# Overlapping one sequence's chunk loop with the MLP of the one before and the in-projection of the next, and decays taken from running sums, in a Mamba-2 and mixture-of-experts layer

## Chip, cores and metric

One Trainium2 chip, one of its cores. The metric is the device time of one execution in microseconds; lower is better. All arrays are float32.

## What is computed

Input: 4 sequences of 512 tokens, 256 features each. Two residual blocks follow each other.

```python
# block 1, per sequence (Mamba-2 mixer, then an MLP with 704 hidden units)
x0 = layernorm(x);  h = rmsnorm(x0) * norm1_w
z, xBC, dt = split(h @ in_proj_w)               # 512, 768, 8 columns
dt  = softplus(dt + dt_bias)
xBC = silu(causal_conv(xBC, 4 taps) + conv_b)   # -> xs (8 heads x 64), B (128), C (128)
dA  = dt * -exp(A_log)
# chunks of 128 tokens:
L      = exp(segsum(dA))                        # 8 heads, 128 x 128, lower triangle
Y_diag = (C B^T * L) @ (xs * dt)
states = B^T @ (xs * dt * exp(A_last - A_cum))  # carried from chunk to chunk
Y_off  = (C @ state) * exp(A_cum)
y  = rmsnorm((Y_diag + Y_off + D * xs) * silu(z)) * mixer_norm_w
h1 = x0 + y @ out_proj_w
x  = x + h1 + (silu(h2 @ gate_w) * (h2 @ up_w)) @ down_w      # h2 = rmsnorm(h1) * norm2_w
# block 2: mixture of experts over all 2048 tokens, 8 experts, the best 2 for each token
x  = x + moe(layernorm(x))
```

## The kernel before

Five instruction streams (TensorE = PE, VectorE = DVE, ScalarE = ACT, GpSimd = POOL, SyncE = SP) are written by hand and meet in semaphores. Each engine works strictly in the order in which its stream is written. Tokens lie in tiles of 128 rows; a sequence has four of them, which are also its four chunks.

Block 1 runs in `body(b)`, once for each sequence, of which the two middle ones are a loop on each engine. Before the first body stands the in-projection of sequence 0 (`hT_`, `dt_`, `xbc_`, `z_`, `dec_` on PE). A body has two halves:

- The **chunk loop** over c = 0 to 3. PE: `seg_` (L434), `front` (transposes L358 and G = B C^T, L424), `off_` (L446, C times state), `back`'s eight products for the heads (L451), its state product (L459), `yT_` (transposes) and `out_` (L476). POOL's `masked_dA` (L1394) makes, for each chunk, a 128 x 1024 array, dA of each head masked by the triangle; `seg_` multiplies it by a triangle of ones, which gives the segment sums of all 8 heads in PSUM banks 4 and 5; ACT's `decay` (L787) takes the exponential into `em`; DVE's `front` (L1041, L1044) masks G and multiplies it in. DVE's `off` (L1050, L1052), `y_` (L1062), `state`, `h1_` (L1082, L1087, L1090) and POOL's `scaled_x` (L1399), `plus_x_D` (L1404), `gated` (L1410), `scale_y` finish the chunk.
- **In-projection of b + 1 and MLP of b.** `hT_`, `dt_` (L374), six `xbc_` (L391), `dec_` (L382), four `z_` (L402), then `h2T`, `mlp_up` (L543, L547, L552) and `mlp_down` (L566). Meanwhile ACT's `tap` and DVE's `conv_taps` (L1026, three instructions for each of 6 blocks) do the convolution, DVE's `dt_softplus` (L1006 to L1019) the softplus, DVE (L1255) the product of gate and up, and DVE's `add_mlp` the residual.

The routing of sequence b - 1 (`xn_`, logits, `route_pick`, `route_slots`, POOL's `scatter`) lies inside body b. The PSUM banks have several uses one after the other: banks 0 and 1 for instance hold z, dt, decays, states, y turned, the output product and the MLP. The experts' weights are loaded by SP: experts 0 and 1 right behind the other weights at the start, into a region of SBUF of their own; 2 to 5 as soon as the last sequence's chunk loop is over; 6 and 7 in block 2.

After block 1 come the last routing steps, the table of tiles, the first gather, and then 39 tiles of block 2 (L701 and L714 on PE, L1318 on DVE), in loops.

Of the kernel before, what the change touches and what calls it, by code (L numbers as in the profile page):

```python
# [7 lines left out]
P = 128  # L8
SEQS, SEQ = 4, 512
TOKENS = SEQS * SEQ  # L10
CH = SEQ // P
# [101 lines left out]
def build(nc, hidden, vecs, consts, empty, in_proj, out_proj, gate_w, up_w, down_w,  # L113
          router_w, w1, w2, w3, out):
    xn_rows = nc.dram_tensor("xn_rows", [TOKENS + P, D], F32).ap()
    lists = nc.dram_tensor("lists", [SLOT_TILES * P, 2], F32).ap()

    ctx = ExitStack()
    with ctx:
# [6 lines left out]
        at = [EARLY * EXPERT]  # L126
# [13 lines left out]

        win = cols(KD, PROJ)
# [3 lines left out]
        xc = cols(CB, SEQ)  # L145
        sz = cols(CH, INNER)
# [4 lines left out]
        bg = cols(2, 2 * P)  # L151
        gm = cols(2, P)
        mda = cols(2, HEADS * P)
        em = cols(2, HEADS * P)
# [17 lines left out]
        xnT = cols(KD, P)  # L172
        junk_h = cols(D)
        dec = cols(3, CH, HEADS)
        dtx, dta, dtu, dtd, dtr, dts, dts2, dtq, dtp, dtl, dtv, dA = (cols(CH, HEADS) for _ in range(12))
        st6 = cols(CH, 6)
        mv = cols(CH, 2)
        ve, rs, rr, t4a, t4b, cur_rs, ssy, ry, vy, ssh, rh, vh, ve2, rs2 = (cols(CH) for _ in range(14))
        cur_mv = cols(CH, 2)
        st6b = cols(CH, 6)  # L180
        mv2 = cols(CH, 2)
        late_end = at[0]
# [9 lines left out]
        ys = cols(D)  # L192
        at[0] = max(at[0], late_end)
# [25 lines left out]
        recg = cols(2 * P)  # L219
# [20 lines left out]


# [4 lines left out]
        cur_kept = sem("cur_kept")  # L246
# [1321 lines left out]
```

## Time and profile before

| | us |
|---|---|
| median of 3 runs | 812.43 |
| lowest, highest | 812.38, 813.51 |
| the profiled execution's own time | 808.96 |
| its span, first to last instruction | 807.1 |
| PE busy | 728.0 (90%) |
| DVE busy | 577.3 (72%) |
| POOL busy | 307.4 (38%) |
| ACT busy | 227.4 (28%) |

The profiled execution took 1.9 us more than its span, and 3.5 us less than the median. A view of the profile by stage gives busy time for each engine in a stretch; the chain of waits follows the last instruction back to what released it. A matmul of float32 shows as two records, a transpose as one. A record's duration holds its fill and drain, so that records overlap, and the distance between starts is the cost of one.

### The profile page before, as it was taken

To read this page: it belongs to the slowest core of one execution; us is meant where nothing else is said; L and a number is where in the kernel's file an instruction comes from. 1 tells how busy PE (TensorE), PEld (TensorE's weight loads), DVE (VectorE), ACT (ScalarE), POOL (GpSimd) and SP (SyncE) were. 2 spreads that over 40 slices of the span, in tenths; PEclk is the share of its full clock that TensorE was granted. 3 is DMA by queue.
4 is the path that set the end of the run, shared out by engine and by line. 5 is a ranking of instruction groups with operands and counts; after the bars stand their busy time and mean duration, and the time that the engine had idled before them with its cause. 6 is when DMAs were issued, how large, how long until landed. Compare 5 with 4: busy or idle time off the path is not lost.

```text
span 807.1 us, 10348 instructions
## 1 busy us (share of the span) xinstructions
PE 728.0 (90%) x2751; PEld 464.5 (58%) x2752; DVE 577.3 (72%) x1370; ACT 227.4 (28%) x482; POOL 307.4 (38%) x505
## 2 busy tenths in 40 slices
PE   5888999899998999979608999999999999999992
PEld 3466547664667547655504666666666666666661
DVE  4686827868477865853634888888888888888870
ACT  1654544544444534631102111111111111111110
POOL 1266203740456315532242333344433344333422
PEclk9999999999999999999758999999999999999997
DMA  9800001000010000038617211111211112111111
GB/s 324 293 2 1 1 0 53 2 0 0 2 52 0 0 0 27 26 120 274 181 31 276 47 32 26 27 26 29 35 28 26 26 26 32 32 26 26 26 15 19
DMA packets 30167, 43.74 MB, mean 54 GB/s; under 512 B 4099, under 2 KB 23875, under 8 KB 30128
## 3 DMA queue, kind: packets, MB, share of 16 engines
q1 hardware_dynamic: 21600, 33.15, 12.3%
q0 software_dynamic: 8544, 10.30, 8.0%
q8 instruction: 12, 0.20, 0.1%
q14 instruction: 11, 0.09, 0.0%
HBM read 33.84 MB, written 9.75 MB: 54 GB/s over the span
## 4 chain that ended last, share of the span: by engine, by line
PE 64%; DVE 11%; issue 9%; POOL 9%; DMA 3%; ACT 2%; DVEq 0%; POOLq 0%; ACTq 0%; SPq 0%
PE ps L701 28%; PE ps L714 14%; PE ps L391 5%; PE ps L402 3%; PE ps L547 3%; PE ps L358 3%; PE ps L552 3%; POOL lists L1426 2%; POOL big L1404 2%; DVE big L1318 2%; PE ps L476 1%; DVE big L1026 1%; PE ps L566 1%; PE ps L434 1%; PE ps L374 1%
## 5 line engine op out<-in xcount | busy, mean ns | idle before, releaser
L1318 DVE STREAM_TRANSPOSE big<-big 32x224 f32<-32x224 f32 x608 | 244.8, 403 | 9.1
L701 PE MATMUL ps<-big 128*128 x624 | 242.7, 542 | 1.1 <-ACT big L932 1.1
L701 PEld LDWEIGHTS ps<-big 128*128 128x128 f32 x624 | 119.0, 191 | 106.1 <-issue 104.1
L1361 POOL TENSOR_TENSOR big<-big 128x1 f32<-128x1 f32 x179 | 56.6, 316 | 280.3 <-DVE big L1326 159.5
L714 PE MATMUL ps<-big 128*128 x546 | 124.5, 380 | 2.1 <-DVE big L1338 1.3
L714 PEld LDWEIGHTS ps<-big 128*128 128x128 f32 x546 | 100.8, 190 | 15.0 <-issue 2.9
L938 ACT ACTIVATE big<-ps 128x896 f32<-128x896 f32 x39 | 35.8, 917 | 217.2 <-PE ps L701 217.2
L358 PE MATMUL ps<-big 128*128 128x128 f32 (+1 forms) x327 | 52.3, 281 | 39.9 <-DMA big<-lists,big 16.0
L358 PEld LDWEIGHTS ps<-big 128*128 128x128 f32 (+1 forms) x327 | 39.8, 144 | 69.6 <-issue 28.6
L1333 DVE TENSOR_TENSOR big<-big,ps 128x896 f32<-128x896 f32 x39 | 42.4, 1087 | 47.5 <-PE ps L701 47.4
L1503 POOL DMA_INDIRECT out_rows<-big x39 | 63.3, 1623 | 23.8 <-issue 23.8
L1026 DVE SCALAR_TENSOR_TENSOR big<-ps,big 128x511 f32<-128x511 f32 (+2 forms) x72 | 52.9, 746 | 11.0 <-ACT big L778 9.4
L391 PE MATMUL ps<-big 128*128 128x512 f32 x96 | 47.6, 634 | 0.8 <-DVE big L1026 0.8
L932 ACT ACTIVATE big<-ps 128x256 f32<-128x256 f32 x39 | 14.9, 383 | 111.6 <-PE ps L358 111.6
L1426 POOL DMA_INDIRECT lists<-big x32 | 31.9, 997 | 37.9 <-DVE big L1159 28.6
L1492 POOL DMA_INDIRECT big<-xn_rows,big x39 | 40.2, 1030 | 5.9 <-issue 0.5
L566 PE MATMUL ps<-big 128*128 128x256 f32 x192 | 42.1, 379 | 0.0
L566 PEld LDWEIGHTS ps<-big 128*128 128x128 f32 x192 | 36.3, 190 | 5.2 <-issue 0.5
L547 PE MATMUL ps<-big 128*128 128x512 f32 x80 | 37.9, 596 | 1.0 <-DVE big L1245 1.0
L552 PE MATMUL ps<-big 128*128 128x512 f32 x80 | 37.6, 592 | 0.0
L451 PEld LDWEIGHTS ps<-big 128*128 128x128 f32 x256 | 31.4, 195 | 8.3 <-issue 6.3
L1399 POOL TENSOR_TENSOR big<-big 128x512 f32<-128x512 f32 x16 | 17.5, 1092 | 48.6 <-ACT big L795 48.6
(173 smaller groups left out, 924.4 us busy)
## 6 DMA issues: line engine op xcount, KB each, us to landing
big<-in_w SPq DMA_DIRECT2D x24, 896.0 KB, 11.8
out_rows<-big SPq DMA_DIRECT2D x4, 512.0 KB
xn_rows<-big SPq DMA_DIRECT2D x4, 512.0 KB
big<-in_hidden SPq DMA_DIRECT2D x1, 1536.0 KB, 11.8
big<-in_in_proj SPq DMA_DIRECT2D x1, 1288.0 KB, 6.9
big<-in_gate SPq DMA_DIRECT2D x1, 640.0 KB, 12.8
big<-in_up SPq DMA_DIRECT2D x1, 640.0 KB, 8.7
big<-in_down SPq DMA_DIRECT2D x1, 640.0 KB, 9.2
```

The source lines that it names most:

```text
L358: return nc.tensor.transpose(out_ap, in_ap, ident[0:n, 0:n])
L391: last = mm(bank(4 + j % 2), win[:, k, INNER + j * P:INNER + (j + 1) * P], hT[:, k, :], start=(k == 0), stop=(k == KD - 1))
L547: last = mm(bank(bk), wgate[:, k, j * P:(j + 1) * P], h2T[:, k, :], start=(k == 0), stop=(k == KD - 1))
L552: last = mm(bank(bk + 1), wup[:, k, j * P:(j + 1) * P], h2T[:, k, :], start=(k == 0), stop=(k == KD - 1))
L566: last = mm(bank(t % 2)[:, 0:D], hid[:, j, t * P:(t + 1) * P], wdown[:, j, :], start=(j == 0), stop=(j == JB - 1))
L701: last = mm(bank(bk + n)[:, 0:HALF], xT[:, k, :], expert_cols(e, off + k * M + n * HALF, HALF), start=(k == 0), stop=(k == KD - 1))
L714: last = mm(bank(7)[:, 0:D], hTs[:, half, j * P:(j + 1) * P], expert_cols(e, 2 * KD * M + j * D, D), start=(j == 0), stop=(j == MB - 1))
L1026: last = V.scalar_tensor_tensor(xc[:, j, s:SEQ], bank(4 + j % 2)[:, 0:SEQ - s], vec[:, w:w + 1], xc[:, j, s:SEQ], ALU.mult, ALU.add)
L1318: last = V.transpose(hTs[c * SQ:(c + 1) * SQ, half, :].rearrange("p (j t) -> p j t", j=MB)[:, :, q * SQ:(q + 1) * SQ], ha[q * SQ:(q + 1) * ...
L1361: G.tensor_tensor(idle[:, k:k + 1], half[:, 0:1], half[:, 0:1], ALU.add)
L1426: G.indirect_dma_start(lists, bass.IndirectOffsetOnAxis(ap=slots[:, t, k:k + 1], axis=0), recs[:, t, k, :], None).then_inc(rec_out, 16)
L1503: G.indirect_dma_start(out, bass.IndirectOffsetOnAxis(ap=sidx, axis=0), ys, None, compute_op=ALU.add, bounds_check=TOKENS + P - 1, oob_is_ ...
```

## The change

**One stage for three things.** All loops over sequences are unrolled. For sequence k each engine runs `both(k)`: the four chunks of k, with the in-projection of k + 1, the MLP of k - 1, the start (`hT_`, `dt_`) of k + 2 and the routing of k - 2 put between their steps. Sequence 0's chunks run with the in-projection of 1 alone; sequence 3's with the MLP of 2; the MLP of 3 is alone. `xc`, `sz`, `em`, `dec`, `dtv` have two copies, for even and odd sequences; the even ones of the first three lie where experts 0 and 1 will be. So SP loads those two only after the last chunk of sequence 2.

**Decays.** `masked_dA` and `seg_` are gone. `dec_` gets a fourth, small product, the running sums of dA transposed. ACT copies them (`cumT`, and `cums` per token), SP's `spread` writes them to DRAM and reads them back into `em`, each head's row into all 128 partitions, 512 KB for a chunk; DVE's new `apart` subtracts the token's own sum and takes the minimum with 0, eight instructions of 128 x 128 for a chunk; then come the exponential and G as before.

**Smaller ones.** G and B turned are made once for a sequence instead of per chunk. POOL multiplies y by silu(z) before the diagonal part arrives; DVE multiplies the diagonal part by silu(z) itself and adds it. `decayed_x` goes from DVE to POOL. PSUM: banks 0 to 2 carry all wide products in turn, 3 and 4 all that is turned, 5 the diagonal part, 6 states, 7 the small ones and `out_`.

```diff
+        STREAM = 3
+        TURN0, TURN1, DIAG, STATES, MISC = 3, 4, 5, 6, 7
...
+            def spread(n):
+                rows = cum_rows[n * CH * HEADS:(n + 1) * CH * HEADS, :]
+                sp.wait_ge(cumT_taken, n + 1)
+                sp.dma_start(rows, cumT[0:CH * HEADS, :]).then_inc(cum_out, 16)
+                sp.wait_ge(cum_out, 16 * (n + 1))
+                if n >= 2:
+                    sp.wait_ge(y_ps, nth(n - 2, CH, CH - 1))
+                for c in range(CH):
+                    sp.dma_start(em[n % 2][:, c, :].unsqueeze(1),
+                                 rows[c * HEADS:(c + 1) * HEADS, :].rearrange("(o h) l -> o (h l)", o=1).unsqueeze(0).to_broadcast([P, 1, HEADS * P])).then_inc(cum_in[c], 16)
...
                 for i, tri in enumerate((tri_after, tri_upto, ones)):
...
+                mm(bank(MISC)[0:CH * HEADS, M_CUM:M_CUM + P], dA.rearrange("p a b -> p (a b)"), tri_upto, start=True, stop=True).then_inc(dec_ps, 1)
...
-            def seg_(b, c, prev):
-
-                pe.wait_ge(mda_ready, nth(b, CH, c))
...
-                for i in range(2):
-                    last = mm(bank(4 + i), tri_after, mda[:, c % 2, i * 512:(i + 1) * 512], start=True, stop=True)
-                last.then_inc(seg_ps, 1)
...
+            def apart(n, c):
+                v.wait_ge(cums_taken, n + 1)
+                v.wait_ge(cum_in[c], 16 * (n + 1))
+                for hh in range(HEADS):
+                    q = slice(hh * P, (hh + 1) * P)
+                    last = V.tensor_scalar(em[n % 2][:, c, q], em[n % 2][:, c, q], cums[:, c, hh:hh + 1], 0.0, ALU.subtract, ALU.min)
+                last.then_inc(apart_ready, 1)
...
+            def y_(n, c):
...
+                V.tensor_tensor(yz, bank(DIAG), sz[n % 2][:, c, :], ALU.mult).then_inc(y_taken, 1)
+                v.wait_ge(y_taken, nth(n, CH, c))
+                v.wait_ge(y3_ready, nth(n, CH, c))
+                V.tensor_tensor(yb[:, c % 2, :], yb[:, c % 2, :], yz, ALU.add).then_inc(y4_ready, 1)
...
-            def masked_dA(n, c):
-                g.wait_ge(dA_ready, nth(n, 1, 0))
...
-                G.tensor_tensor(heads(mda[:, c % 2, :]), tri_upto.unsqueeze(1).to_broadcast([P, HEADS, P]),
-                                over_head(dA[:, c, :], P), ALU.mult).then_inc(mda_ready, 1)
...
+            def decayed_x(n, c):
...
+                G.tensor_tensor(heads(xdtd[:, c % 2, :]), heads(xdt[:, c % 2, :]), over_head(dec[n % 2][:, 0, c, :]), ALU.mult).then_inc(xdtd_ready, 1)
```

PE's order in the middle of a chunk loop, before (inside `body`, chunks 1 and 2; L446 is `off_`, L451 the heads' products, L459 the state, L476 `out_`, L434 `seg_`, L494 logits):

```order
L446 MATMUL ps<-big 128x512
L451 MATMUL ps<-big 128x64 x8
L456 REGISTER_ALU
L459 MATMUL ps<-big 128x512
L476 MATMUL ps<-big 128x256 x4
L428 REGISTER_ALU
L434 MATMUL ps<-big 128x512 x2
L491 REGISTER_ALU
L494 MATMUL ps<-big 128x8 x2
```

The same place in the changed kernel, `both(1)` at chunk 2 (L514 is `off_`, L525 the heads' products, L539 the state, L682 and L691 `mlp_up` of sequence 0, L405 transposes, L582 `out_`):

```order
L514 MATMUL ps<-big 128x512
L525 MATMUL ps<-big 128x64 x8
L539 MATMUL ps<-big 128x512
L682 MATMUL ps<-big 128x512 x2
L691 MATMUL ps<-big 128x512 x2
L682 MATMUL ps<-big 128x512 x2
L691 MATMUL ps<-big 128x512 x2
L405 MATMUL ps<-big 128x128 x8
L682 MATMUL ps<-big 128x512 x2
L691 MATMUL ps<-big 128x512 x2
L582 MATMUL ps<-big 128x256 x4
```

`seg_` is gone, and products of the MLP, which before stood behind the whole loop, lie between the chunk's dependent steps.

DVE's order at chunks 0 and 1 of sequence 0, before (L1041 and L1044 mask G and multiply it in, L1059 and L1062 are `y_`, L1067 `state`, L1078 `decayed_x`, L973 to L980 statistics of the next sequence, L1050 and L1052 `off`):

```order
L1041 TENSOR_TENSOR big<-big 128x128
L1044 TENSOR_TENSOR big<-big 128x1024
L1059 TENSOR_TENSOR big<-big,ps 128x512
L1067 COPY big<-ps 128x512
L1078 TENSOR_TENSOR big<-big 128x512
L973 BN_STATS big<-big 128x6 x4
L959 MEMSET big 128x1
L977 BN_AGGR big<-big 128x2 x4
L980 TENSOR_SCALAR big<-big 128x4
```

The same place now (L1404 is `apart`, L1384 `conv_taps` of sequence 1, L1434 and L1437 `y_`, L1442 `state`, L1415 multiplies G in):

```order
L1404 TENSOR_SCALAR big<-big 128x128 x8
L1384 SCALAR_TENSOR_TENSOR big<-ps,big 128x511
L1384 SCALAR_TENSOR_TENSOR big<-ps,big 128x510
L1384 SCALAR_TENSOR_TENSOR big<-ps,big 128x509
L1434 TENSOR_TENSOR big<-ps,big 128x512
L1437 TENSOR_TENSOR big<-big 128x512
L1442 COPY big<-ps 128x512
L1415 TENSOR_TENSOR big<-big 128x1024
```

Between chunk steps DVE now does the convolution of the next sequence and eight small instructions for each chunk.

## Rows read from the trace of the kernel before

**Rows 1.** The page: the span, and busy time of each engine.

```profile
span 807.1 us, 10348 instructions
PE 728.0 (90%) x2751; PEld 464.5 (58%) x2752; DVE 577.3 (72%) x1370; ACT 227.4 (28%) x482; POOL 307.4 (38%) x505
```

**Rows 2.** Busy time by stage: stretch, its length, each engine, granted clock, DMA share, GB/s.

```profile
11.50:37.60 26.10, 22.79 (x70) 11.46 (x71) 17.53 (x37) 11.89 (x20) 6.03 (x6) 0.93 0.99 346
37.60:76.90 39.30, 33.08 (x168) 23.40 (x169) 29.12 (x49) 22.22 (x64) 25.24 (x29) 0.96 0.01 1
76.90:169.00 92.10, 87.05 (x362) 56.20 (x363) 59.68 (x123) 43.26 (x100) 32.03 (x38) 0.98 0.04 12
169.00:260.30 91.30, 86.14 (x367) 55.52 (x367) 64.85 (x159) 43.34 (x101) 40.88 (x47) 1.00 0.04 12
260.30:358.80 98.50, 92.27 (x382) 59.77 (x382) 66.00 (x151) 43.90 (x105) 38.32 (x46) 0.98 0.06 18
```

**Rows 3.** The chain that ended last, in time: start, length, instructions.

```profile
76.92 1.92 PE ps L374 x16
80.66 1.73 PE ps L476 x8
88.20 3.43 PE ps L391 x8
95.07 0.87 PE ps L358 x8
116.55 1.73 PE ps L434 x4
...
254.00 1.73 PE ps L451 x16
```

**Rows 4.** DVE's groups from 37.6 to 358.8: count, busy us, mean ns, idle before.

```profile
L1044 DVE TENSOR_TENSOR big<-big 128x1024 f32<-128x1024 f32 x16 | 21.9, 1370 | 0.6
L1062 DVE TENSOR_TENSOR big<-big,ps 128x512 f32<-128x512 f32 x12 | 8.3, 688 | 15.7 <-POOL big L1404 15.7
L1082 DVE TENSOR_SCALAR big<-big 128x256 f32<-128x256 f32 x8 | 6.1, 768 | 0.0
```

**Rows 5.** Timeline of DVE, stretches of sequence 0: start, length, instructions.

```profile
10.02 1.38 DVE L986 TENSOR_SCALAR big<-big 128x256 f32<-128x256 f32 x4 [3.70 <-POOL big L1387]
...
16.16 0.18 DVE L1006 TENSOR_SCALAR big<-big 128x32 f32<-128x32 f32 x1 [0.30 <-ACT big L768]
...
19.66 4.53 DVE L1026 SCALAR_TENSOR_TENSOR big<-ps,big 128x511 f32<-128x511 f32 x6
...
59.30 1.13 DVE L1082 TENSOR_SCALAR big<-big 128x256 f32<-128x256 f32 x1
```

**Rows 6.** Timeline at 318 to 350, DVE and POOL.

```profile
319.62 1.89 POOL L1394 TENSOR_TENSOR big<-big 128x1024 f32<-128x1024 f32 x1
319.72 3.63 DVE L1099 TENSOR_SCALAR big<-big 128x256 f32<-128x256 f32 x4 [1.00 <-DVE big L1203]
...
349.89 0.41 DVE L1082 TENSOR_SCALAR big<-big 128x256 f32<-128x256 f32 x1
```

**Rows 7.** POOL's groups from 37.6 to 358.8.

```profile
L1410 POOL TENSOR_TENSOR big<-big 128x512 f32<-128x512 f32 x16 | 20.3, 1268 | 11.9 <-PE ps L434 6.0 <-DVE big L1059 5.9
L1404 POOL TENSOR_TENSOR big<-big 128x512 f32<-128x512 f32 x12 | 18.2, 1518 | 22.0 <-DVE big L1050 19.8 <-ACT big L807 2.2
```

**Rows 8.** DMA issues of the first 60 us: KB each, median us to landing.

```profile
q1 hardware_dynamic: 8496, 12.43, 59.0%
big<-in_w SPq DMA_DIRECT2D x6, 896.0 KB, 11.8
```

**Rows 9.** Timeline of PE and POOL behind the last chunk loop.

```profile
358.84 1.09 PE L358 MATMUL ps<-big 128*128 128x128 f32 x8 [0.53 <-DVE big L1239]
...
375.84 1.07 POOL L1426 DMA_INDIRECT lists<-big  x1 [18.23 <-DVE big L1159]
...
425.88 1.85 PE L701 MATMUL ps<-big 128*128 x2 [0.57 <-ACT big L932]
```

More of the change, by code:

```diff
@@ L666, in _ @@
-            over_seqs(pe, body)
-            pe.wait_ge(gate_taken, SEQS * JB)
-            pe.wait_ge(down_taken, SEQS * CH)
+            bg_(0)
+            front(0, 0)
+            hT_(1)
+            dt_(1)
+            front(0, 1)
+            xbc_(1, 0)
+            dec_(1)
+            xbc_(1, 1)
+            diag(0, 0)
+            state_(0, 0)
+            xbc_(1, 2)
+            off_(0, 1)
+            diag(0, 1)
+            state_(0, 1)
+            xbc_(1, 3)
+            front(0, 2)
@@ new lines, in _ @@
+            xbc_(1, 4)
+            yT_(0, 0)
+            xbc_(1, 5)
+            out_(0, 0)
+            off_(0, 2)
+            diag(0, 2)
+            state_(0, 2)
+            z_(1, 0)
+            front(0, 3)
+            z_(1, 1)
+            yT_(0, 1)
+            z_(1, 2)
+            out_(0, 1)
+            off_(0, 3)
+            diag(0, 3)
+            bg_(1)
+            z_(1, 3)
+            yT_(0, 2)
+            hT_(2)
+            out_(0, 2)
+            dt_(2)
+            front(1, 0)
@@ new lines, in _ @@
+            positions(0)
+            mlp_up(2, 2)
+            xnT_(1, 0)
+            front(3, 3)
+            mlp_up(2, 3)
+            logits(1, 0)
+            yT_(3, 1)
+            off_(3, 3)
+            diag(3, 3)
+            out_(3, 1)
+            xnT_(1, 1)
+            mlp_up(2, 4)
+            logits(1, 1)
+            yT_(3, 2)
+            mlp_up(2, 5)
+            out_(3, 2)
+            mlp_down(2, 0)
+            yT_(3, 3)
+            mlp_down(2, 1)
+            out_(3, 3)
@@ L920, in _ @@
+            gate(3, 2)
+            route_exp(2)
+            for j in range(3, JB):
+                gate(3, j)
             for part, (n, ts) in enumerate(HALVES):
                 q = slice(ts.start * P, ts.stop * P)
[L922 to L923 removed]
+                act.wait_ge(xnT_ps, (SEQS - 1) * (CH // 2) + 1 + part)
+                A(h2T[:, :, q], bank(TURN0, 2).rearrange("p (k n) -> p k n", k=KD)[:, :, q], ACT.Copy).then_inc(xnT_taken, 1)
@@ new lines, in _ @@
+            conv_taps(1, 1)
+            off(0, 1)
+            y_(0, 1)
+            state(0, 1)
+            conv_taps(1, 2)
+            scores(0, 3)
+            conv_taps(1, 3)
+            h1_(0, 0)
+            conv_taps(1, 4)
+            off(0, 2)
+            y_(0, 2)
+            state(0, 2)
+            conv_taps(1, 5)
+            apart(1, 0)
+            ln1_stats(2)
+            h1_(0, 1)
+            apart(1, 1)
+            off(0, 3)
+            y_(0, 3)
+            masked_G(1)
@@ new lines, in _ @@
+            both(1)
+            both(2)
+            y_(3, 0)
+            state(3, 0)
+            add_mlp(1, 2)
+            add_mlp(1, 3)
+            h1_(2, 3)
+            ln2_stats(1)
+            scores(3, 2)
+            h2(2)
+            xn_(1)
+            off(3, 1)
+            y_(3, 1)
+            state(3, 1)
+            h2T1(2)
+            scores(3, 3)
+            hidden_(2, 0)
+            h1_(3, 0)
+            hidden_(2, 1)
+            off(3, 2)
+            y_(3, 2)
+            state(3, 2)
```

1432 lines of the change are left out of this document (880 added, 552 removed).

## Prediction

> **What bounds the kernel now.** I read the page first: PE is busy 90% of the span, every other engine 72% or less [rows 1]. Then the stages. From the start of one sequence's `dt_` to the next one's take 92.1 and 91.3 us, with PE busy in 87 and 86 of them, DVE in 60 to 65 and POOL in 32 to 41; the last such stretch takes 98.5 us [rows 2]. So PE bounds block 1 in the middle, but not at the start: in the first chunk loop (37.6 to 76.9) it is busy 33 of 39 us. Block 2 begins at 425.88 [rows 9], takes the other 381 us, and is not touched. The change can win only ahead of it.
>
> Busy is not work, so I count PE's products from the chain's rows [rows 3]. Four wide products (8 records of L391) take 3.43 us, so 0.86 each; four of 128x256 (L476) 1.73, so 0.43; eight transposes 0.87; `dt_` 1.92; the eight heads' products 1.73; a `seg_` 1.73. A sequence then needs: in-projection 20 x 0.86 = 17.2; gate and up 22 x 0.86 = 18.9; down 24 x 0.43 = 10.3; `seg_` 6.9; off and state 6 x 0.86 = 5.2; heads 7.0; `out_` 16 x 0.43 = 6.9; 60 transposes 6.5; G 0.9; `dt_`, logits and small ones 4.9. Together 84.7 us. PE starts `hT_` at 11.5 and begins the last `h2T` at 358.8. In between lie four sequences less the last MLP and routing: 4 x 84.7 - 33.4 = 305.4, so up to 316.9. The other 42 us are waits and slow stretches; 3.6 of them are filled with dummy products.
>
> **What the change does to PE.** `seg_` goes: 4 x 6.9 = 27.6 us, all of it on the engine that bounds. The fourth product of `dec_` adds 0.2 a sequence. Logits and positions of sequence 2 move behind the last `h2T` (3.1). By stage, the new order holds: up to the start of `both(1)` 68.0 us of work, `both(1)` 69.6, `both(2)` 74.8, the stage of sequence 3 with MLP 2 62.8, dummies 3.7. From 11.5 with no wait at all, that is 290.4.
>
> **What it does to DVE.** The reverse. New are 128 instructions of `apart`. The trace has none of this shape; the nearest are four of 128x256 in 1.38 us, 0.345 each [rows 5], and 32-wide ones at about 0.2. Half the columns cannot take longer than 0.345 and hardly less than 0.1; I take 0.2, nearer to the short ones, so 1.6 a chunk, and 1.8 with some waiting for POOL: 7.2 a sequence. The ends are 0.8 and 2.8 a chunk. The Trainium skill (VectorE: DVE Perf Modes, section on the TRN2 errata) speaks against such small pieces: each pays a fixed latency, and it advises tiles of 512 elements or more. With its measured 150 cycles and a halved pass, an estimate of 0.22 each, the sum per chunk would be 1.8 before any waiting, 3 us more over the sixteen. Further, `y_` becomes two instructions: 0.6 more, four times. Masking G once saves about 1.2, `decayed_x` on POOL 3.1.
>
> The wait inside `y_` grows. Today DVE stands 15.7 us in 12 chunks behind POOL's `plus_x_D` [rows 4], 1.3 each. Now `gated` (1.27 [rows 7]) comes ahead of the addition too, and 0.6 of it is covered by the product with silu(z): 1.3 + 1.27 - 0.6, about 1.9, for three chunks a sequence. Queued behind it on DVE are the state, the next `conv_taps` and with them PE's next `xbc_`.
>
> **Stage of sequence 0.** Here DVE becomes the bound. From its first tap at 19.7 [rows 5] to `both(1)` it has: 12 blocks of taps at 2.3 (six taps in 4.53 [rows 5]) 27.6; 8 `apart` 14.4; 6 multiplications by G at 1.25 (mean 1.37 [rows 4], less beside a freer POOL) 7.5; `y_` 5.6; states 1.8; `off` 3.4; three `h1_` at 1.9 5.7; two sets of statistics and h 7.2; two of hT, dt and softplus (3.5 from 16.16 to 19.66 [rows 5], and 1.1) 9.2; masking 1.4. Sum 83.8. Waits: three in `y_` 5.7; for G at about 40, for `dt_(1)` at about 46, and between early taps some 6. So DVE comes to `both(1)` at 115. PE's last things there (`dt_(2)`, `front`) stand some 9 ahead of DVE's, so PE enters at 106, not at 11.5 + 68.
>
> **Later stages.** In `both(1)` DVE has 67.5 with its waits (taps 13.8, `apart` 7.2, G 5.0, `y_`, states and off 10.8, `h1_` 7.6, gate times up 3.9, the rest 13.5, waits 5.7), in `both(2)` 68.3. PE has more, so it bounds, but both run dense in fixed orders; I give PE 5, 4 and 5 us of waits in the three stages, against 7 in a sequence today (91.7 - 84.7). PE: 106 + 74.6 + 78.8 + 67.8 + 3.7 = 330.9 for the last `h2T`, against 358.8: 27.9 us earlier.
>
> **Behind it.** From `h2T` to block 2 took 67.1 us [rows 9]. Logits and positions of 2 add 3.1. `route_slots(2)` moves behind the fifth block of the MLP, so POOL's eight scatters of sequence 2 (first at 375.84 [rows 9], 17 us after `h2T`, about 1.26 apart) start about 8 later and end just as the last layernorm wants POOL: 2 more. So +5, and block 2 begins 22.9 earlier.
>
> **Costed at nothing, with the cover.** The round trip of `spread`: 16 KB out, 4 x 512 KB in. The first 60 us carry 12.43 MB, of which six issues of 896 KB are experts 0 and 1, now gone from there [rows 8]. The other 7 MB at 346 GB/s [rows 2] are through by about 24; the first chunk's sums land near 29 and the fourth near 35, and DVE reaches `apart(0, 0)` at 32. Were they 5 later, taps 4 and 5 would wait behind it, and so would G. The experts' load now falls in sequence 3's stage, where the queue is idle (1% to 6% [rows 2]), 19 us of it in 66. ACT's load hardly changes (44 of 92).
>
> Sum: span 807.1 - 22.9 = 784.2; with the 1.9 around it 786.1. Against the median, which lies 3.5 above the profiled execution: **789.5**.
>
> **Rivals.**
> 1. *DVE keeps up* (0.17). `apart` at the low end (0.8 a chunk, 8 less in stage 0), PE with waits of 2 per stage: 98 + 71.6 + 76.8 + 64.8 + 3.7 = 314.9; with +5 the gain is 38.9: 773.5. For it: PE's orders now always have independent products between dependent steps. Against: DVE's 84 us in stage 0.
> 2. *The waits stay* (0.18). In-order streams this dense wait for each other; 9 us per stage instead of 5: 343.9, gain 9.9: 802.5. For it: the longer chain through POOL.
> 3. *DVE and POOL hold each other* (0.10), which ends slower. Four 128x256 `tensor_scalar` that take 1.38 alone took 3.63 beside POOL's L1394 and its neighbours, and L1082 0.41 in one place, 1.13 in another that began while POOL worked [rows 5, 6]; its mean is 0.77 [rows 4], 0.36 above. If each of `apart`'s instructions pays 0.36, stage 0 grows by 64 x 0.36 = 23, `both(1)` and `both(2)` by 11.5 each, of which 7 and 10.5 are covered by PE's larger load: 28 us, minus 22.9: 818. It decides from about 0.31 an instruction. Against: eight pieces follow each other, POOL works a third of the time and loses its longest instruction (2 us, sixteen times). The Trainium skill (SBUF — State Buffer, Who interferes with whom) has the rule: the port pair that VectorE shares with GpSimd is an exclusive lock held for a whole instruction, and `tensor_scalar` is among those that take it. By that rule the trace agrees with 3.63 against 1.38; I stay with a small share, since the lock delays one piece per POOL instruction and not all.
> 4. *It does not do what it says* (0.05): the sums land late or a bank's reader holds PE, and it ends within a few us of 812 or above.
>
> **Chances.** Forecast 0.50, for 779 to 799. A measurement of this kernel tells 0.2% (1.6 us) from no change. Slower: rival 3 and most of 4, 0.13; same: 0.03; faster: 0.84. The range 768 to 808 takes in the forecast, rivals 1 and 2 and their edges; the rest, about 0.2, is rival 3, 4, and a still better fit.
>
> **What would show it.** Right: no L434 and no POOL 128x1024 in the new trace; `apart` near 0.2 a piece; first `dt_` of sequence 2 near 103; last `h2T` near 331; DVE over 85% busy before 115, PE over 90% after. DVE idle ahead of `y_`'s addition near 1.9. Wrong: `apart` pieces with a mean of 0.5 (rival 3), DVE idle for `cum_rows` (rival 4), the last `h2T` below 320 (rival 1) or block 2 longer than 381 us.

## The result, and the profile after

| | before | after |
|---|---|---|
| median, us | 812.97 (4 runs) | 854.69 (4 runs, 850.53 to 859.43) |
| profiled execution, its span | 808.96, 807.1 | 855.37, 853.6 |
| PE busy | 728.0 (90%) | 726.9 (85%) |
| first `dt_` of sequences 1, 2, 3 | 76.9, 169.0, 260.3 | 46.1, 116.2, 198.7 |
| last `h2T` | 358.8 | 383.9 (forecast 330.9) |
| start of block 2 | 425.9 | 472.1 (forecast 403) |

The changed kernel takes 1.0512 times as long (95% interval 1.0454 to 1.057): 42 us slower, where 23 us faster was forecast. Block 2 takes 381.6 us, as before (381.2). All of the loss lies ahead of it: in the two profiled executions, which are 46 us apart and not 42, it is 25 us up to the last `h2T` and 21 behind it. The profiled execution of the kernel before, 808.96, is the fastest of all its executions on record; the others took 812 to 819.

The page's first lines:

```profile
span 853.6 us, 9996 instructions
PE 726.9 (85%) x2695; PEld 468.5 (55%) x2696; DVE 585.7 (69%) x1457; ACT 225.9 (26%) x470; POOL 285.5 (33%) x475
```

Busy time by stage of the changed kernel, columns as in [rows 2]. The stretches are the in-projection of sequence 0, its chunks, `both(1)`, `both(2)`, the stage of sequence 3, the tail and block 2:

```profile
11.30:35.30 24.00, 23.06 (x72) 11.60 (x72) 19.35 (x53) 10.68 (x18) 5.29 (x10) 0.93 0.69 239
35.30:119.70 84.40, 58.96 (x250) 39.42 (x250) 58.05 (x137) 39.20 (x87) 23.62 (x26) 0.87 0.08 26
119.70:203.80 84.10, 76.49 (x309) 48.24 (x308) 61.66 (x142) 42.94 (x103) 26.83 (x31) 0.95 0.08 26
203.80:291.30 87.50, 80.96 (x324) 52.38 (x324) 57.64 (x132) 39.81 (x94) 23.55 (x26) 0.94 0.11 37
291.30:384.00 92.70, 74.90 (x317) 54.21 (x318) 45.52 (x131) 26.31 (x68) 33.92 (x38) 0.87 0.22 77
384.00:472.00 88.00, 43.64 (x164) 29.16 (x164) 32.34 (x161) 13.47 (x23) 28.68 (x36) 0.72 0.70 147
472.00:853.60 381.60, 364.79 (x1253) 230.47 (x1253) 306.69 (x687) 52.03 (x79) 140.58 (x301) 0.98 0.20 41
```

Two things stand in these rows. Length less PE's busy time is PE's idle time: 0.9 + 25.4 + 7.6 + 6.5 + 17.8, 58 us up to the last `h2T`. By [rows 2] it was 26 in the kernel before. And the granted clock is 0.87, 0.95, 0.94 and 0.87 in the four stages. A stage in which PE is busy for 59.0 us at 0.87 has lost up to (1 - 0.87) x 59.0 = 8 us to the lower clock; the four lose 8, 4, 5 and 10, with 2 for the first row some 28 us. By [rows 2] the same sum was about 7.

The two explain most of where the last `h2T` stands. At the unit costs of [rows 3] PE's work from 11.3 to 384 is 279 us; PE was busy for 314, 35 more. In the kernel before the work was 309 and PE was busy for 321, 12 more. So PE has 30 us less work than before (27.6 of it `seg_`), 32 more idle and 23 more busy time beyond its work: +25, as measured. Of the 23, the lower clock can account for up to 21 (28 less 7). The fall of the clock is not chance of one execution: over the whole span it was 0.912 to 0.925 in all eight executions of the changed kernel on record, and 0.953 to 0.965 in the 42 of the kernel before whose clock is recorded.

What the slow running looks like, in stretches of 5 us of the changed kernel, same columns:

```profile
45.00:50.00 5.00, 3.88 (x20) 3.91 (x21) 1.59 (x6) 1.21 (x2) 0.28 (x1) 0.65 0.00 0
115.00:120.00 5.00, 3.81 (x18) 3.84 (x19) 1.62 (x5) 0.51 (x2) 0.00 (x0) 0.50 0.00 0
120.00:125.00 5.00, 4.19 (x20) 3.42 (x18) 4.86 (x14) 4.47 (x12) 3.33 (x3) 0.50 0.00 2
205.00:210.00 5.00, 5.00 (x17) 3.88 (x17) 4.65 (x12) 3.24 (x10) 3.35 (x3) 0.50 0.00 0
```

0.50 is the lower of TensorE's two levels, 1.2 of 2.4 GHz. In 205 to 210 PE is busy for all of the 5 us and does about half the work: the state's two products (L539) take 2.02 us there and 1.12 at 142.9. The busy share alone doesn't show that. The same in PE's timeline, `dt_` of sequences 1, 2 and 3:

```profile
46.12 3.24 PE L432 MATMUL ps<-big 128*128 128x8 f32 x16 [3.27 <-issue]
116.19 3.55 PE L432 MATMUL ps<-big 128*128 128x8 f32 x16 [3.98 <-DVE big L1454]
198.67 1.92 PE L432 MATMUL ps<-big 128*128 128x8 f32 x16 [0.18 <-issue]
```

The sixteen small products take 1.92 us where nothing is ahead of them, as in [rows 3], and 3.24 and 3.55 behind gaps of 3.27 and 3.98 us. The gap need not be that long: the slow stretch from 203 to 210 follows idle times of 0.77 and 1.50 us, and that from 292 to 299 one of 1.41, while the clock stayed at 1.00 behind gaps of 2.24 (at 37.5) and 1.84 us (at 142.9). Up to the last `h2T` there are ten such stretches, in the kernel before four.

DVE's groups from 11 to 440, columns as in [rows 4], and then its waits and PE's (waited for: us in total, times, longest):

```profile
L1404 DVE TENSOR_SCALAR big<-big 128x128 f32<-128x128 f32 x128 | 30.6, 312 | 0.0
L1437 DVE TENSOR_TENSOR big<-big 128x512 f32<-128x512 f32 x16 | 11.1, 692 | 32.1 <-POOL big L1896 32.0
```

```profile
DVE big L1437 <- POOL big L1896: 32.0, 12, 12.0
```

```profile
PE ps L539 <- DVE big L1424: 12.5, 5, 5.5
PE ps L622 <- ACT big L1057: 9.7, 1, 9.7
PE ps L639 <- DVE big L1521: 5.5, 1, 5.5
PE ps L472 <- DVE big L1384: 5.4, 6, 1.3
PE ps L444 <- DVE big L1377: 4.1, 1, 4.1
```

`apart` (L1404) is busy 30.6 us in sixteen chunks, 1.9 each, where the working had 1.8. The wait inside `y_` (L1437 for POOL's `gated`, L1896) is 32.0 in 12 chunks; less its one long wait of 12.0, 1.8 a chunk, where the working had 1.9. PE waits for many things, a few us each. No wait for the sums' way through DRAM shows.

The long wait is the last stage's. POOL and PE there:

```profile
343.00 1.20 POOL L1920 DMA_INDIRECT lists<-big  x1 [0.27 <-issue]
...
352.16 0.97 POOL L1920 DMA_INDIRECT lists<-big  x1 [0.30 <-issue]
353.16 1.27 POOL L1884 TENSOR_TENSOR big<-big 128x512 f32<-128x512 f32 x1
354.57 1.26 POOL L1896 TENSOR_TENSOR big<-big 128x512 f32<-128x512 f32 x1
```

```profile
346.94 1.88 PE L691 MATMUL ps<-big 128*128 128x512 f32 x4
358.55 1.87 PE L622 MATMUL ps<-big 128*128 128x8 f32 x8 [9.73 <-ACT big L1057]
```

POOL issues the eight scatters of sequence 0's lists (343.0 to 353.1) ahead of `plus_x_D(3, 3)`. DVE's last `y_`, ACT's copy and PE stand behind them.

The tail, SP's queue and POOL's waits at its end:

```profile
385.63 1.49 SPq L325 DMA_DIRECT2D big<-in_w  x2
...
407.54 0.88 SPq L325 DMA_DIRECT2D big<-in_w  x2
...
421.50 0.88 SPq L325 DMA_DIRECT2D big<-in_w  x2
...
441.52 0.88 SPq L325 DMA_DIRECT2D big<-in_w  x2
442.44 0.47 SPq L327 DMA_DIRECT2D big<-in_w  x1
442.95 6.18 SPq L355 DMA_DIRECT2D out_rows<-big  x1
```

```profile
460.93 0.96 POOL L1984 DMA_INDIRECT big<-lists,big  x1 [12.97 <-DMA lists<-big]
467.19 0.18 POOL L1994 CAST big<-big 128x1 int32<-128x1 f32 x1 [5.30 <-DMA big<-lists]
```

Each SP issue of an expert waits until the expert before has landed. They now start 22, 14 and 20 us apart; in the kernel before, between the loads and scatters of its own tail, 9.4, 9.9 and 15.6. The last scatter's data were awaited 12.97 us (before 6.34), the table of tiles 5.30 (before 0.66). Behind that second wait stands a store: those of sequence 3 (L355, L360) stand in SP's queue behind expert 5, and the read of the table waits for them. The end of the chain of waits:

```profile
449.18 16.11 DMA xn_rows<-big
465.34 1.69 DMA big<-lists
467.91 2.79 DMA big<-xn_rows,big
```

The last scatter's data were there more than 4 us before this store had landed (POOL's wait for them ends at 460.9). In the kernel before, the chain ended with the last scatter, 7.00 us to landing. Why expert 2 took 20 us is open: from 400 to 407.5 it was still awaited, while the DMA engines were busy 1% or less of the time.

### The profile page after: what moved, and what is told of

Same layout as the page of the kernel before. It is cut to its first block, busy times and chain, and to the rows that moved or that the text cites. A ratio compares the mean times of both kernels' runs of the same rounds, so it can differ in the third digit from the quotient of the medians.

```text
span 853.6 us, 9996 instructions
## 1 busy us (share of the span) xinstructions
PE 726.9 (85%) x2695; PEld 468.5 (55%) x2696; DVE 585.7 (69%) x1457; ACT 225.9 (26%) x470; POOL 285.5 (33%) x475
## 4 chain that ended last, share of the span: by engine, by line
PE 64%; DVE 11%; issue 9%; DMA 6%; POOL 5%; ACT 3%; SPq 1%; DVEq 0%; POOLq 0%; ACTq 0%
PE ps L930 26%; PE ps L943 13%; DVE big L1384 3%; PE ps L682 3%; PE ps L691 3%; PE ps L705 3%; PE ps L405 3%; PE ps L458 3%; PE ps L525 2%; DMA big<-in_w 2%; PE ps L582 2%; DMA xn_rows<-big 2%; PE ps L472 2%; DVE big L1803 1%; PE ps L539 1%
## 5 line engine op out<-in xcount | busy, mean ns | idle before, releaser
L930 PEld LDWEIGHTS ps<-big 128*128 128x128 f32 x624 | 119.3, 192 | 106.4 <-issue 104.5
L1846 POOL TENSOR_TENSOR big<-big 128x1 f32<-128x1 f32 x153 | 48.5, 317 | 203.1 <-DVE big L1811 161.6
L943 PEld LDWEIGHTS ps<-big 128*128 128x128 f32 x546 | 100.8, 190 | 14.9 <-issue 2.9
L405 PE MATMUL ps<-big 128*128 128x128 f32 (+1 forms) x327 | 57.4, 291 | 49.0 <-DMA big<-lists,big 24.8
L405 PEld LDWEIGHTS ps<-big 128*128 128x128 f32 (+1 forms) x327 | 43.9, 153 | 82.6 <-issue 40.2
L1384 DVE SCALAR_TENSOR_TENSOR big<-ps,big 128x511 f32<-128x511 f32 (+2 forms) x72 | 53.7, 747 | 1.9
L458 PE MATMUL ps<-big 128*128 128x512 f32 x96 | 51.1, 664 | 1.3 <-DVE big L1384 1.3
L1872 POOL TENSOR_TENSOR big<-big 128x512 f32<-128x512 f32 x16 | 21.0, 1310 | 80.2 <-ACT big L1029 80.1
L705 PE MATMUL ps<-big 128*128 128x256 f32 x192 | 45.4, 392 | 0.0
L705 PEld LDWEIGHTS ps<-big 128*128 128x128 f32 x192 | 37.8, 199 | 7.6 <-issue 2.5
L525 PEld LDWEIGHTS ps<-big 128*128 128x128 f32 x256 | 35.3, 215 | 10.9 <-issue 10.9
L682 PE MATMUL ps<-big 128*128 128x512 f32 x80 | 39.0, 611 | 0.9 <-issue 0.9
L1884 POOL TENSOR_TENSOR big<-big 128x512 f32<-128x512 f32 x12 | 17.7, 1476 | 65.2 <-DVE big L1424 65.2
```

What stands on the lines that cost most here:

```text
L405: return nc.tensor.transpose(out_ap, in_ap, ident[0:n, 0:n])
L458: last = mm(bank(xbc_bank(n, j)), win[:, k, INNER + j * P:INNER + (j + 1) * P], hT[:, k, :], start=(k == 0), stop=(k == KD - 1))
L525: last = mm(bank(DIAG)[:, hh * HD:(hh + 1) * HD], em[n % 2][:, c, hh * P:(hh + 1) * P], xdt[:, c % 2, hh * HD:(hh + 1) * HD], start=True, ...
L682: last = mm(bank(gate_bank(n, j)), wgate[:, k, j * P:(j + 1) * P], h2T[:, k, :], start=(k == 0), stop=(k == KD - 1))
L705: last = mm(bank(down_bank(n, t))[:, 0:D], hid[:, j, t * P:(t + 1) * P], wdown[:, j, :], start=(j == 0), stop=(j == JB - 1))
L930: last = mm(bank(bk + n)[:, 0:HALF], xT[:, k, :], expert_cols(e, off + k * M + n * HALF, HALF), start=(k == 0), stop=(k == KD - 1))
```

## Experiments

Fifteen runs on four chips, each beside the kernel before on the same chip. The changed kernel itself was timed twice, 1.0512 and 1.0472 (second time: 1.0436 to 1.0508), so single edits are held against their mean, 1.049; under half a point is not told apart from nothing. The landmarks come from the one profiled execution of each; ahead of any edit they differ by up to 2 us (`dt_` of 2 is at 116.2 to 118.4 in the runs that change nothing before it).

| run | median, us | ratio to before (95%) | `dt_` of 2 | last `h2T` | block 2 |
|---|---|---|---|---|---|
| changed kernel, first | 854.69 | 1.0512 (1.0454, 1.057) | 116.2 | 383.9 | 472.1 |
| changed kernel, again | 854.52 | 1.0472 (1.0436, 1.0508) | 116.3 | 383.9 | 469.0 |
| 1 stores first | 852.58 | 1.0456 (1.043, 1.0483) | 118.4 | 386.1 | 471.0 |
| 2 scatter late | 849.95 | 1.0433 (1.0398, 1.0467) | 117.5 | 373.1 | 466.4 |
| 3 one head apart | 846.87 | 1.0371 (1.0328, 1.0414) | 112.2 | 378.4 | 465.1 |
| 4 `y_` as before | 843.72 | 1.0354 (1.0329, 1.0378) | 108.5 | 373.3 | 456.3 |
| 5 lists first | 846.61 | 1.0372 (1.0341, 1.0402) | 117.6 | 385.8 | 463.9 |
| 6 dummies | 848.29 | 1.0386 (1.0353, 1.042) | 117.7 | 380.2 | 467.0 |
| 8 state later | 859.99 | 1.0536 (1.0482, 1.059) | 117.4 | 390.3 | 477.2 |
| kernel before | 812.97 | 1 | 169.0 | 358.8 | 425.9 |
| 9 before, half `seg_` | 812.89 | 0.9967 (0.9946, 0.9988) | 174.5 | 362.1 | 430.7 |
| 2 + 4 + 5 | 828.67 | 1.0146 (1.0107, 1.0184) | 114.5 | 368.0 | 448.8 |
| 2 + 4 + 5 + 6 | 824.73 | 1.009 (1.0053, 1.0126) | 113.3 | 361.0 | 441.2 |
| those and 3 | 816.08 | 0.9996 (0.9973, 1.0018) | 109.2 | 354.2 | 434.3 |
| 13 `apart` on ACT | 870.88 | 1.0701 (1.0666, 1.0737) | 115.3 | 400.8 | 484.5 |
| 2 + 4 + 5 + 6 + 13 | 841.87 | 1.0337 (1.0304, 1.037) | 114.8 | 380.9 | 461.1 |
| and the tail's scatter | 840.74 | 1.0337 (1.0298, 1.0376) | 109.9 | 376.1 | 454.1 |

### What was `seg_` worth?

Kernel before, with `seg_`'s second product of 512 columns left out, so that the decays of four heads are stale:

```diff
-                for i in range(2):
+                for i in range(1):
                     last = mm(bank(4 + i), tri_after, mda[:, c % 2, i * 512:(i + 1) * 512], start=True, stop=True)
```

> The kernel BEFORE, with only the first of the two products of each segment sum (part of the computation is left out): 16 wide products fewer, 13.8 us of TensorE at full clock. My forecast took all segment sums as time of the engine that bounds. If that holds: 12 to 14 us less than before, 799 to 801. If the chunk loop is set by a chain through other engines: under 6 us less, 807 to 813.

Sixteen products of 0.86 us go, 13.8 us. The time falls by 0.33% (0.12 to 0.54), 2.7 us: a fifth, or 7 to 32% by the interval. Its stages, from the first `dt_` of one sequence to the next one's, to be read against [rows 2]:

```profile
79.90:174.50 94.60, 86.95 (x354) 56.80 (x355) 60.61 (x123) 43.49 (x100) 32.22 (x38) 0.95 0.04 12
174.50:264.90 90.40, 83.88 (x359) 55.24 (x359) 64.91 (x159) 43.52 (x101) 41.34 (x47) 0.98 0.04 12
```

In the second row PE is busy 2.3 us less than in the kernel before, DVE and ACT the same, and the stage only 0.9 shorter. In the first, PE is as busy as before with 3.5 us less to do, the granted clock is 0.95 instead of 0.98, and the stage is 2.5 longer. Two things take the removed time back: waits, and the clock. The clock is seen in all executions: its median is 0.949 in the ten of this run and 0.957 in the thirteen beside it, an estimate of up to 0.008 x 815 = 6.5 us more of slow running. So PE's time was not what the chunk loop lasts, and `seg_` also kept the clock up. How the rest of the 11 us divides, and through which engines the chain of waits goes, the run does not show. (The trace kept of the kernel before is of its fastest execution, that of this run of a middling one, so whole landmarks of the two are not compared.)

### VectorE's eight small instructions

```diff
-                for hh in range(HEADS):
+                for hh in range(1):
                     q = slice(hh * P, (hh + 1) * P)
                     last = V.tensor_scalar(em[n % 2][:, c, q], em[n % 2][:, c, q], cums[:, c, hh:hh + 1], 0.0, ALU.subtract, ALU.min)
```

The sums of seven heads are not subtracted.

> The changed kernel, with the subtraction done for the first of eight heads only (part of the computation is left out): 112 of 128 small VectorE instructions are gone, 27 us of its busy time. Theory A (VectorE's load sets the stages): 15 to 27 us less, 828 to 840. Theory B (latency from engine to engine and the clock that falls in the gaps set them): under 8 us less, 847 to 853.

Ratio 1.0371, 1.2 points less. `dt_` of 2 comes 4 us earlier, `dt_` of 3 5.1 earlier (193.6), the last `h2T` 5.5: most of the gain is in the stage of sequence 0, although 1.6 us a chunk go from every stage. DVE's time counts there and hardly elsewhere, as forecast. But it does not bound that stage in full: of the 13 us taken out of it (eight chunks' worth), some 4 come back, a third.

Moved instead of left out:

```diff
             def decay(n, c):
...
+                for hh in range(HEADS):
+                    q = slice(hh * P, (hh + 1) * P)
+                    last = A(em[n % 2][:, c, q], em[n % 2][:, c, q], ACT.Relu, scale=-1.0, bias=cums[:, c, hh:hh + 1])
+                last.then_inc(apart_ready, 1)
+                act.wait_ge(apart_ready, nth(n, CH, c))
-                A(em[n % 2][:, c, :], em[n % 2][:, c, :], ACT.Exp).then_inc(decays, 1)
+                A(em[n % 2][:, c, :], em[n % 2][:, c, :], ACT.Exp, scale=-1.0).then_inc(decays, 1)
```

> The changed kernel, with apart moved whole from VectorE to ScalarE: eight Relu instructions of 128x128 per chunk (each head, with the token's sum as bias), then the exponential with scale -1. The same result, only on an engine with room. Theory that VectorE's time bounds the stage of sequence 0 alone: as leaving seven of the eight out, 4 to 7 us less, all before both(1), ratio 1.035 to 1.042. Rival, that the place of the work in the chain counts and not the engine (the exponential now comes 2 us later behind the sums): no gain, or slower, 1.047 to 1.055.

Slower by 2.1 points: the rival, and beyond it. ScalarE in this run, its timeline near 46 us, and PE's waits from 11 to 390:

```profile
46.60 2.44 ACT L1024 ACTIVATE big<-big 128x128 f32<-128x128 f32 x8
49.06 1.06 ACT L1027 ACTIVATE big<-big 128x1024 f32<-128x1024 f32 x1
```

```profile
PE ps L582 <- ACT big L1059: 8.4, 2, 5.7
PE ps L405 <- ACT big L1035: 7.0, 3, 5.6
PE ps L405 <- ACT big L1039: 3.6, 1, 3.6
```

ScalarE is busy 26% of the span, but it turns all transposed tiles over to PE, in order. With 2.4 us put ahead of those copies, PE waits for three of them 19 us in six places, where it waited 6 us for the same ones in the changed kernel (L1053, L1029, L1033), and the last `h2T` comes 17 us later. ScalarE's table loads (ACT_TABLE_LOAD, 1.28 us each) don't explain it: up to 390 there are eleven, against twelve in the changed kernel. An engine with time to spare is not an engine with a free place.

### The order of `y_`

```diff
-                V.tensor_tensor(yz, bank(DIAG), sz[n % 2][:, c, :], ALU.mult).then_inc(y_taken, 1)
...
-                V.tensor_tensor(yb[:, c % 2, :], yb[:, c % 2, :], yz, ALU.add).then_inc(y4_ready, 1)
+                    V.tensor_tensor(yb[:, c % 2, :], yb[:, c % 2, :], bank(DIAG), ALU.add).then_inc(y_taken, 1)
...
+                g.wait_ge(y_taken, nth(n, CH, c))
+                G.tensor_tensor(yb[:, c % 2, :], yb[:, c % 2, :], sz[n % 2][:, c, :], ALU.mult).then_inc(y4_ready, 1)
```

DVE adds the diagonal part, and POOL gates afterwards, behind `scaled_x` and `decayed_x` of the next chunk.

> The changed kernel, with y put together as before: VectorE adds the diagonal part to y once POOL has added x times D, POOL multiplies by silu(z) afterwards. VectorE has one instruction fewer per chunk and waits for one POOL instruction instead of two. If VectorE's 32 us of waiting for POOL's gate set the pace: 8 to 15 us less, 840 to 847. If the chain behind y (turning, output product, h1) sets it, that chain is no shorter and the time stays at 854, or grows by up to 5.

Ratio 1.0354, 1.4 points less, the largest of the single edits. DVE's wait for POOL here is 25.1 in 12 chunks instead of 32.0, DVE has one instruction of 0.69 us fewer a chunk, and every instruction behind moves up; `dt_` of 2 comes 7.7 us earlier. The run does not tell the shorter wait from the missing instruction. The wait had the size that was forecast. That it would cost nothing beyond the stage of sequence 0 had not been worked out, but taken from PE's larger load.

### POOL's scatters in the last stage

```diff
-                if k == 3:
-                    scatter(0)
...
             scale_h(3)
+            scatter(0)
             scatter(1)
```

> The changed kernel, with POOL's eight scatters of sequence 0 moved from the middle of sequence 3's chunk loop to behind the last scale. Theory A (POOL in order): they held plus_x_D of the last chunk from 343 to 353, and behind it TensorE, which stood still 9.7 us and fell to half clock: 10 to 14 us less, about 842. Theory B: 24 scatters now fall in the tail beside the experts' loads and give the gain back: 850 to 856.

The gap of 9.7 us is gone, and the last `h2T` stands at 373.1, 10.8 earlier. The ratio falls by 0.6 points only (its interval overlaps that of the unedited kernel's second timing), less than half of that, since the tail grows from 88.1 to 93.3 us. The end of this run's chain shows where:

```profile
376.35 32.61 DMA big<-in_w
450.11 9.50 DMA xn_rows<-big
459.67 1.68 DMA big<-lists
```

Expert 2, now loaded beside sixteen scatters instead of eight, lands after 32.61 us instead of 20.36; experts 3 to 5 and the stores stand behind it in SP's queue, and the table is read only after them. The last scatter itself was in 11 us before that store.

### The tail

> The changed kernel, with SP's order in the tail altered: experts 2 and 3 are issued, then the stores of sequence 3's rows, then experts 4 and 5. Theory A (in order queue): the stores wait behind the issue of expert 5, which waits for expert 3's landing; they were issued at 442.95 although the last down product ended at 422. Then block 2 starts about 18 us earlier: about 836 to 838 us. Theory B (DMA bandwidth): the late loads of experts fill the DMA engines and would delay the stores and lists as much in any order: no change, about 854.

```diff
-            for e in range(EARLY, SOON):
-                load_next(e)
+            load_next(EARLY)
+            load_next(EARLY + 1)
             store_x1(3)
             store_xn(3)
+            for e in range(EARLY + 2, SOON):
+                load_next(e)
```

> The changed kernel, with experts 4 and 5 issued only once the lists and the first two gathers are in; experts 2 and 3 and the stores stay ahead. The order of the stores alone gained 2 us, because the last scatter then landed after 13.0 us beside the experts' loads, where it took 7.0 in the kernel before. Theory A (scatters and expert loads slow each other on the same DMA engines): the last scatter lands in about 7 us and the lists come 1 us after, so block 2 begins 6 to 9 us earlier, 843 to 848 in all. Theory B (the tail's length is set by the engines' chain alone): 850 to 854.

```diff
-            for e in range(EARLY, SOON):
-                load_next(e)
+            load_next(EARLY)
+            load_next(EARLY + 1)
             store_x1(3)
             store_xn(3)
...
-            for e in range(SOON, E):
+            for e in range(EARLY + 2, E):
                 load_next(e)
```

With the stores alone moved ahead of experts 4 and 5, they go out 15 us sooner, and what is gained is within the noise (1.0456, the tail 84.9): the store no longer ends the chain, but the last scatter does, 76 us behind the last `h2T` where the store landed 81 behind it, since beside the experts' loads the scatter still took 12.95 us to land. With both experts behind the first gather as well, it took 8.29, and the tail was 78.2 instead of 88.1: 1.0372, 1.2 points less. What this tail waits for, once the stores are out of the way, is a small scatter, and the bulk loads in flight slow it.

### The clock

38 dummy products of 128x256 on PE in front of the gaps at `dt_` of 1 and 2, `dec_(1)` and `diag(k, 0)`, for instance:

```diff
             hT_(2)
             out_(0, 2)
+            pe.wait_ge(z_taken, nth(1, CH, 1))
+            keep_warm(xbc_bank(2, 0), 9)
             dt_(2)
```

> The changed kernel with 38 dummy products of 128x256 (16 us of TensorE at full clock) put where it stood idle: ahead of dt_ of sequences 1 and 2 and dec_ of 1, and ahead of the first head products of sequences 1 to 3. Theory A (the granted clock falls to 1.2 GHz in these gaps and the slow products behind them are about half of the missed time): the products behind run at 2.4 GHz, 5 to 18 us less, 836 to 849. Theory B (the gaps are waits for other engines, and what TensorE does behind them is waited for by nobody): same or slower by up to 6.

Ratio 1.0386, 1.0 points less, for products that compute nothing. `dt_` of 2 takes 1.92 us instead of 3.55, and the stages around it, with PE's clock:

```profile
36.00:121.00 85.00, 67.79 (x308) 47.23 (x307) 58.46 (x147) 39.89 (x91) 23.01 (x27) 0.92 0.08 26
121.00:205.00 84.00, 78.03 (x319) 49.21 (x320) 61.29 (x136) 41.54 (x101) 27.17 (x31) 0.96 0.08 26
```

0.92 instead of 0.87. The first of these is no shorter for it: `dt_` of 2 is at 117.7, as in runs 5 and 8 on the same chip, so PE's slow running there is not what that stage waits for. What is gained comes later. Over the whole span the clock is 0.934 to 0.936 in all four executions.

### An order that let PE go on

`state_` one wide product later in each chunk, since PE waits 12.5 us there for DVE's `off` (L539 for L1424):

```diff
-            state_(0, 1)
             xbc_(1, 3)
+            state_(0, 1)
```

> The changed kernel with the state product of chunks 1 and 2 put behind the next independent product on TensorE (five places written out, seven executed), since TensorE waited 12.5 us in 5 places for VectorE's scaling of the product with the state. If those waits are lost time: 5 to 10 us less, 844 to 849. If VectorE, which needs the state next, then waits in TensorE's place: within 3 of 854.

1.0536, no gain. PE's wait of 12.5 us fell to 1.5, and DVE waited in its place: 2.9 us for the state, and 26.4 instead of 17.8 for `out_`. No block of products is only filler here.

### Together

> The changed kernel itself once more, unedited, so that the three kernels beside it have their base on the same chip. Its ratio to the kernel before should lie between 1.042 and 1.057, where it and its relatives have stood.

> The changed kernel with three edits at once: POOL's scatter of sequence 0 behind the last stage's chunk steps, y_ gated after the diagonal part as in the kernel before, and the lists' scatters ahead of experts 4 and 5. Alone they gave -0.8, -1.5 and -1.4 points of the ratio (from 1.0512). If the three causes are separate, the sum is near 1.014. If they are one cause told three ways (the last stage's scatters fall out of the tail, or the tail refills), less than 2.5 points come off: 1.026 or more.

> The three edits and the 34 wide dummy products in front of the known gaps of PE (alone -1.3 points). Separate causes: 1.002 or below, so that what is left of the change is no gain and no loss, the 27.6 us of seg_ paid back by the clock and by waits. If the dummies' gain came from the gaps that y_ left, then no more than 0.5 points on top of the three edits.

> All four, and of apart one head's instruction of eight per chunk, so that the subtraction of the sums is left out for seven heads. Alone it gave -1.4 points, all in the stage of sequence 0. Theory that VectorE bounds only there: 5 to 9 us less than with the four edits (-0.6 to -1.1 points), in the stage of sequence 0. Theory that VectorE bounds every stage once the other waits are gone: 12 us or more less, spread over the stages.

The three edits come to 1.0146, 3.3 points under the changed kernel on the same chip; singly they made 0.6 + 1.4 + 1.2 = 3.2. So these are separate causes. The dummies add 0.6 on top instead of 1.0 (the intervals just touch): part of what they gave was in gaps that the edits had closed, and 1.002 was not reached. Seven eighths of `apart` add 0.9, within the 0.6 to 1.1 expected, but not only in the stage of sequence 0: `dt_` of 2 comes 4.1 us earlier than with the four, `dt_` of 3 6.4 (187.8 against 194.2), the last `h2T` 6.8. Then the kernel is level with the one before, with most of the subtraction left out.

> The four edits that together stood at 1.009, and apart on ScalarE. With seven of eight left out they stood at 0.9996. Expected near that: 0.998 to 1.004. If ScalarE's own queue becomes the wait (its taps and copies stand behind eight more instructions a chunk), above 1.009.

> As the one before, and POOL's scatter of sequence 2 behind both halves of the last layernorm's scale instead of ahead of it. In the trace of the four edits POOL is in those scatters until 403, while the statistics were there at 398.2, and idle from 406.8 to 416. Theory that POOL's order holds the tail: 3 to 6 us less, -0.4 to -0.7 points, so 0.992 to 0.999, at or below the kernel before. Rival, that the list's last transfer sets it anyway: no difference.

```diff
             scatter(1)
-            scatter(2)
             for n, ts in HALVES:
                 ln2_scale(n, ts)
+            scatter(2)
```

The four edits with `apart` on ScalarE: 1.0337, 2.5 points worse than without it, as in the single run. POOL's order in the tail on top of that: the tail takes 78.0 us instead of 80.2, a gain of 2 where 3 to 6 were expected, and the ratio does not move. The two traces already differ by 5 us ahead of the edit, so this stays unresolved.

The best version that computes all of it is the one with four edits, 1.009. None was found that beats the kernel before.

## Why the prediction was wrong

Forecast 789.5, measured 854.7: 65 us. The landmarks miss by 69; the forecast's median stood 3.5 above its profiled execution, the measured one 0.7 below. For each stage, the miss splits into PE's busy time beyond its work at unit costs and PE's idle time beyond the idle time in the forecast:

| stage | forecast | measured | busy beyond work | idle beyond forecast |
|---|---|---|---|---|
| up to the start of `both(1)` | 106 | 119.7 | 14.0 | -0.1 |
| `both(1)` | 74.6 | 84.1 | 6.9 | 2.6 |
| `both(2)` | 78.8 | 87.5 | 6.2 | 2.5 |
| the last stage | 71.5 | 92.7 | 8.4 | 12.8 |
| tail | 72.1 | 88.1 | | |

- **"`seg_` goes: 27.6 us, all of it on the engine that bounds."** This step failed. The work did go, but not the time: PE's busy time fell by 7 us and its idle time rose by 32. PE was busy 94% in the middle of the kernel before, and the reading from "busiest" to "bounds" was not tested: half of `seg_` taken from that kernel gives a fifth of its time. Of the forecast's 27.9 us of gain, most stood on this.
- **The clock, not in the sum at all.** This is the largest part of the miss up to the last `h2T`: 35 of 53 us are busy time beyond unit costs, of which the lower clock can account for up to 28. The unit costs came from rows at full clock. The working names slow stretches among the 42 us of the kernel before, and gives the new order none. That order has six gaps of 3 to 10 us in PE, and behind each PE ran at half rate. The dummies show that about 1 point of the ratio can be had back. How much of the rest is lost time, and how much slow work beside other waits, stays open; in the stage of sequence 0 a better clock did not make the stage shorter.
- **PE's waits, 5, 4 and 5 us a stage.** By the rows they are 7.6, 6.5 and 17.8. The first two were nearly right in size. The third misses the eight scatters on POOL, of which the working counted those of sequence 2 in the tail and forgot those of sequence 0, which the change puts ahead of the last `plus_x_D`; experiment 2 confirms their 10 us.
- **DVE bounds the stage of sequence 0, PE the others.** Half right. Experiment 3 gains mostly in that stage, but only a third of what it takes out of it. Of the signs that the prediction named, two did not come: DVE was busy 71.6 of the 95.3 us from its first tap at 19.7 to 115, 75% where over 85 was forecast, and PE 88% from `both(1)` to the last `h2T`, where over 90 was. The price of `apart` (1.8 a chunk) and the wait of `y_` (1.9) were right to a tenth (1.9 and 1.8). The Trainium skill (VectorE: DVE Perf Modes, section on the TRN2 errata) gave the prediction an estimate of 0.22 us a piece; the eight follow each other at about 0.24. The stage was 13.7 longer than summed. DVE waited in it 4.3 us for PE's `out_` ahead of `h1_`, 3.9 for the heads' products and 3.4 for `dt_`, and PE's `dt_(2)` waited 3.98 for `h1_`: a circle that a sum of one engine's load does not hold. The working names the wait at `dt_(1)` and one for G, and its sum to 115 has no term for them. Which of these waits makes the stage that long, no run separates.
- **Tail: +5.** It was +21. Ten of it stands ahead of the last scatters (POOL's last group of four starts 59.3 us behind `h2T` instead of 49.4), for the logits, the routing and the scatters of sequences 1 and 2; eleven behind, in transfers that landed late beside the experts: the last scatter, and the store of `xn` that stands behind expert 5. That experts 4 and 5 would still be loading there was not asked, although their load hangs on the chunk loop's end in both kernels.
- **The round trip of `spread` costs nothing.** Right: no wait on it.
- **Rivals.** Number 3, slower at 818 by port conflicts, had the sign but not the cause: `apart`'s pieces took 0.312 us against the 0.31 from which it decides, yet with a pitch of 0.24 they cost what the forecast said (half of them took 0.28 or less, the longest 1.30). Number 2, "the waits stay", had the cause in part, priced at 4 us a stage. Nothing in the list combined waits and clock. The range's upper end, 808, took in rival 2's waits and no slow running.

## What to carry to other kernels

An engine that is 90% busy is not thereby the bound: before pricing work that is removed from it, take a part of that work out and see what share of its time comes back (here a fifth of it for PE, and a third for DVE in the stage where it was thought to bound). When three loops are woven into one, the waits don't add as each engine's load does: every in-order engine becomes a relay between the others, so look for what is queued behind each new wait, scatters and stores included. And price PE's gaps twice, once as idle and once as the slow products that follow them.

## What of the hardware was not expected

- **The price of a gap.** Behind every idle stretch of 3 to 10 us, and behind some of 1.4 to 2.7, TensorE was granted its lower level: 16 small products 3.55 us instead of 1.92, a clock of 0.50 for 205 to 210 with PE busy throughout, and 0.87 over whole stages. The Trainium skill (TensorE: Matmul & The Clock Gate, section What's actually happening) calls the penalty of the ramp less than 1% of a typical kernel span. Here the clock falls again and again, and up to the last `h2T` alone it can cost up to 28 us, 3% of 854; 38 dummy products bring back 1.0 point.
- **Products that held the clock up.** With half of `seg_` gone, the kernel before ran at a median clock of 0.949 instead of 0.957, and gained a fifth of what was removed.
- **Small scatters and bulk loads.** The last scatter landed in 12.95 us beside experts' loads and in 8.29 with two experts fewer. In the other direction the first expert of the tail landed after 8.5 us with no scatter beside it (kernel before), 20.4 beside eight and 32.6 beside sixteen.
- **ScalarE's small instruction.** Eight of 128x128 follow each other at 0.30 us (2.43 together), against 0.24 on VectorE.
